# Feed-forward loop: gate and up groups alternate, both sums opened first, silu one unit later, one bank's scaling moved

## What is computed

```python
x = x + tanh(g_xattn) * xattn(layernorm(x), ctx, ctx, Wq, Wk, Wv, Wo, bo, g)
x = x + tanh(g_ffn) * ffn(layernorm(x), ...)
def ffn(x):                          # Wg, Wu: 512 x 1376, Wd: 1376 x 512, from 4-bit words
    gate, up = x2 @ Wg, x2 @ Wu      # w[k, n] = (q[k, n] - z[k // 128, n] - 1) * s[k // 128, n]
    return ((gate * sigmoid(gate) * up) @ Wd).astype(float16)
```

## Time and profile before

| | us |
|---|---|
| median of 3 runs (lowest, highest) | 684.23 (682.98, 684.38) |
| profiled execution, its own time | 683.05 |
| its span, first to last instruction | 681.3 |
| first gate job of unit 0, from the span's start | 410.24 |
| unit 2's first job | 421.84 |
| last gate or up job | 668.23 |

### The profile page before, as it was taken

The page is one execution under the profiler, slowest core; times in us unless marked ns, Lnnn a source line. Parts: engine busy times, 40 slices in busy tenths (PEclk is TensorE's granted clock), DMA queues, the critical chain, the costliest instruction groups (busy, mean ns, idle before and its releaser), DMA issues.

```text
span 681.3 us, 14346 instructions
## 1 busy us (share of the span) xinstructions
PE 662.0 (97%) x5097; PEld 341.9 (50%) x5097; DVE 586.5 (86%) x807; ACT 494.9 (73%) x872; POOL 257.9 (38%) x352
## 2 busy tenths in 40 slices
PE   7899999999999999999999998999999999999996
PEld 6454555455456455545645543444444444444443
DVE  7777898898889889889887948999979988998897
ACT  4886677678677667767866746877787877777774
POOL 6213323223232332322326364554434444444442
PEclk8999999999999999999999999999999999999999
DMA  4112330430332222032021000000000001000102
GB/s 116 37 51 55 99 82 22 102 96 8 97 95 51 53 81 79 7 84 79 10 79 22 7 8 1 1 1 0 1 32 31 1 0 46 18 0 17 43 4 62
DMA packets 30619, 28.58 MB, mean 42 GB/s; under 512 B 18623, under 2 KB 20810, under 8 KB 30578
## 3 DMA queue, kind: packets, MB, share of 16 engines
q1 hardware_dynamic: 28170, 27.37, 14.9%
q10 hardware_dynamic: 2408, 0.70, 0.4%
HBM read 22.06 MB, written 4.23 MB: 39 GB/s over the span
## 4 chain that ended last, share of the span: by engine, by line
PE 87%; ACT 5%; DVE 5%; issue 1%; POOL 1%; SPq 0%; DMA 0%; DVEq 0%; POOLq 0%
PE pair L1364 9%; PE small L1081 8%; PE small L1047 8%; PE pair L1153 8%; PE pair L1365 7%; PE pair L1033 6%; PE pair L1378 6%; PE pair L1387 6%; ACT eq L695 4%; PE small L1065 4%; PE small L1364 4%; PE small L1365 4%; PE pair L1178 3%; PE pair L1012 3%; PE small L1119 3%; PE pair L1163 2%
## 5 line engine op out<-in xcount | busy, mean ns | idle before, releaser
L1767 DVE SCALAR_TENSOR_TENSOR acc<-pair,scale_T,acc 128x512 f32<-128x512 f32 (+1 forms) x176 | 131.5, 748 | 17.6 <-ACT acc L830 5.0
L1378 PE MATMUL pair<-in_hi,d_int 128*128 128x512 f32 (+1 forms) x176 | 100.8, 575 | 0.6 <-ACT in_hi L845 0.5
L1387 PE MATMUL pair<-in_lo,d_int 128*128 128x512 f32 (+1 forms) x176 | 100.2, 573 | 0.0
L686 ACT ACTIVATE ek<-pair,kneg 128x512 f32<-128x512 f32 x128 | 86.5, 683 | 18.0 <-DVE kneg L1627 17.9
L594 POOL TENSOR_TENSOR inter<-act_gate,acc 128x512 f32<-128x512 f32 (+1 forms) x43 | 54.9, 1276 | 109.4 <-DVE acc L1767 104.0
L1364 PE MATMUL pair<-ek,w_gu 128*128 128x512 f16 (+1 forms) x235 | 91.3, 388 | 2.0 <-DVE acc L1767 1.3
L1365 PE MATMUL pair<-ekT,w_gu 128*128 128x512 f16 (+1 forms) x235 | 89.0, 379 | 0.0
L1632 DVE TENSOR_TENSOR eq<-eq,pair 128x1024 f32<-128x1024 f32 x64 | 77.8, 1216 | 11.1 <-PE pair L1138 10.8
L1622 DVE TENSOR_REDUCE qmax<-pair 128x16 f32<-128x1024 f32 x64 | 78.2, 1222 | 8.4 <-PE pair L1012 7.2
L856 ACT ACTIVATE pair<-pair,rescale 128x512 f32<-128x512 f32 x131 | 81.9, 661 | 0.8 <-PE pair L1387 0.8
L1627 DVE TENSOR_REDUCE kneg<-pair 128x2 f32<-128x1024 f32 x64 | 77.9, 1218 | 0.7 <-PE pair L1033 0.7
(11 more groups left out here) (198 smaller groups left out, 1346.2 us busy)
## 6 DMA issues: line engine op xcount, KB each, us to landing
xall<-in_x SPq DMA_DIRECT2D x16, 256.0 KB, 2.8
ctx_raw<-in_ctx SPq DMA_DIRECT2D x16, 256.0 KB, 3.0
out_x<-xall SPq DMA_DIRECT2D x16, 256.0 KB, 2.0
zero<-zeros_plus SPq DMA_DIRECT2D x8, 344.0 KB, 5.6
packed<-in_L_ffn_gate_qweight SPq DMA_DIRECT2D x4, 688.0 KB
packed<-in_L_ffn_up_qweight SPq DMA_DIRECT2D x4, 688.0 KB
packed<-in_L_ffn_down_qweight SPq DMA_DIRECT2D x10, 256.0 KB
zero<-zeros_plus SPq DMA_DIRECT2D x5, 256.0 KB, 4.6
```

What stands on the lines that cost most here:

```text
L686: act.activation(ek[:, b, t, :], k_pairs[t % 2][:, b, :], ACT.Exp, bias=kneg[:, b, t:t + 1], scale=-1.0, accum_out=ksum[:, k_slot(b, t):k_ ...
L1378: pe.matmul(z_bank[nt], d_int[0:w, it, nt * P:(nt + 1) * P], in_hi[0:w, n % 2, :], start=it == 0, stop=False, skip_group_check=True)
L1387: pe.matmul(z_bank[nt], d_int[0:w, it, nt * P:(nt + 1) * P], in_lo[0:w, n % 2, :], start=False, stop=True, skip_group_check=True).then_inc ...
L1767: dve.scalar_tensor_tensor(out=acc[0:w, n % 2, m, :], in0=gu_bank[(8 * n + job) % 3][0:w, :], scalar=scale_T[0:w, it, 4 * m + g:4 * m + g ...
```

## The change

On TensorE and VectorE the jobs alternate between gate and up (`g, m` instead of `m, g`), so that jobs 0 and 1 are the two that open a sum and jobs 2 to 7 are additions, each waiting for the addition two jobs before. ScalarE opens both sums first, then makes silu of the unit before (one unit later than it did), then bank 0, in_hi, banks 1 and 3. Bank 2 goes to VectorE in every unit. In the code that runs before the loop nothing changes; the semaphores' counts are adapted.

```diff
@@ -62,35 +62,14 @@
     return min(P, INTER - it * P)
 
 
-def vector_extra(n):
-
-    j, it = divmod(n, IT)
-    return j > 0 and 3 <= it < 3 + TPC
-
-
-def act_scales(n):
-
-    return BANKS if vector_extra(n + 3) else ACT_BANKS
-
-
-def act_scaled(n):
-
-    return sum(len(act_scales(m)) for m in range(n))
-
-
-def dve_scaled(n):
-
-    return NJ * n - act_scaled(n)
-
-
 def bank_products(n, nt):
 
     return NJ * n + (LAST_LOWS if n == UNITS - 1 else BANKS).index(nt) + 1
 
 
-def groups_done(n, job):
-
-    return 6 * n + job - (job > GH)
+def sums_done(n, job):
+
+    return 6 * n + job - 1
 
 
 def at_least(p, n):
@@ -307,13 +286,13 @@
 
             last = n - UNITS + 2
             if last >= 0 and nt in ((3, 2), (0, 2))[last]:
-                eng.wait_ge(z_dve, dve_scaled(UNITS - 2) + 2 * last + ((3, 2), (0, 2))[last].index(nt) + 1)
+                eng.wait_ge(z_dve, UNITS - 2 + 2 * last + ((3, 2), (0, 2))[last].index(nt) + 1)
             elif last >= 0:
-                eng.wait_ge(z_act, act_scaled(UNITS - 2) + 2 * last + ((0, 1), (3, 1))[last].index(nt) + 1)
-            elif nt in act_scales(n):
-                eng.wait_ge(z_act, act_scaled(n) + act_scales(n).index(nt) + 1)
+                eng.wait_ge(z_act, 3 * (UNITS - 2) + 2 * last + ((0, 1), (3, 1))[last].index(nt) + 1)
+            elif nt == 2:
+                eng.wait_ge(z_dve, n + 1)
             else:
-                eng.wait_ge(z_dve, dve_scaled(n) + 1)
+                eng.wait_ge(z_act, 3 * n + ACT_BANKS.index(nt) + 1)
 
         block = st.enter_context(nc.Block())
 
@@ -822,17 +801,17 @@
 
                 it = n % IT
                 w = width(it)
-                act.wait_ge(gu_mm, 8 * n + GH * m + 1)
+                act.wait_ge(gu_mm, 8 * n + m + 1)
                 if n >= 2 and m == 0:
                     act.wait_ge(gs_ready, n - 1)
                 elif n >= 2:
                     act.wait_ge(inter_ready, n - 1)
-                act.activation(acc[0:w, n % 2, m, :], gu_bank[(8 * n + GH * m) % 3][0:w, :], ACT.Copy,
+                act.activation(acc[0:w, n % 2, m, :], gu_bank[(8 * n + m) % 3][0:w, :], ACT.Copy,
                                scale=scale_T[0:w, it, 4 * m:4 * m + 1]).then_inc(s0_done, 1)
 
             def silu(n):
                 w = width(n % IT)
-                act.wait_ge(acc_done, 6 * n + 3)
+                act.wait_ge(acc_done, sums_done(n, 6))
                 if n:
                     act.wait_ge(inter_ready, n)
                 act.activation(act_gate[0:w, :], acc[0:w, n % 2, 0, :], ACT.Silu).then_inc(gs_ready, 1)
@@ -871,29 +850,30 @@
 
             for n in range(UNITS):
                 open_sum(n, 0)
+                open_sum(n, 1)
+                if n:
+                    silu(n - 1)
                 if late_input(n - 1):
                     transposed(late_input(n - 1))
-                if n:
-                    high_part(n - 1)
-                else:
+                if n == 0:
                     transposed(5)
                     transposed(6)
-                open_sum(n, 1)
+                    transposed(7)
+                if n == 1:
+                    step(PAIRS + 1, PAIRS // 2, 1, False, False, True, drain=True)
                 if n == 2:
                     act.wait_ge(ss_mm, PAIRS)
                     act.activation(ss_rows[:, :], small[1][:, 0:P], ACT.Copy).then_inc(ss_evac, 1)
                 bank_scaled(n - 2, 0)
-                silu(n)
-                if n == 0:
-                    transposed(7)
-                if n == 1:
-                    step(PAIRS + 1, PAIRS // 2, 1, False, False, True, drain=True)
+                if n:
+                    high_part(n - 1)
+                bank_scaled(n - 2, 1)
+                bank_scaled(n - 2, 3)
                 if n == 2:
                     act.activation(ident16[:, :], ident[:, :], ACT.Copy).then_inc(ident16_made, 1)
-                for nt in act_scales(n - 2)[1:]:
-                    bank_scaled(n - 2, nt)
                 if n in NORMALISED_IN:
                     ffn_normalised(NORMALISED_IN.index(n) + 2 * TPC)
+            silu(UNITS - 1)
             bank_scaled(UNITS - 2, 0)
             high_part(UNITS - 1)
             bank_scaled(UNITS - 2, 1)
@@ -1347,7 +1327,7 @@
             def gate_up(n, job):
 
                 j, it = divmod(n, IT)
-                w, (m, g) = width(it), divmod(job, GH)
+                w, (g, m) = width(it), divmod(job, 2)
                 if n == 0 and job == 0:
                     pe.wait_ge(w_int, PAIRS - 2)
                 if it == 0 and job == 0:
@@ -1355,10 +1335,10 @@
                 count = 8 * n + job
                 if count >= 3:
                     n_was, job_was = divmod(count - 3, 8)
-                    if job_was % GH == 0:
-                        pe.wait_ge(s0_done, 2 * n_was + job_was // GH + 1)
+                    if job_was < 2:
+                        pe.wait_ge(s0_done, 2 * n_was + job_was + 1)
                     else:
-                        pe.wait_ge(acc_done, groups_done(n_was, job_was))
+                        pe.wait_ge(acc_done, sums_done(n_was, job_was))
                 lhsT = w_gu[:, m, g, it * P:it * P + w]
                 rows = slice(j * CHUNK, (j + 1) * CHUNK)
                 pe.matmul(gu_bank[count % 3][0:w, :], lhsT, xT_hi[:, g, rows], start=True, stop=False)
@@ -1758,12 +1738,12 @@
 
             def add_group(n, job):
                 it = n % IT
-                w, (m, g) = width(it), divmod(job, GH)
+                w, (g, m) = width(it), divmod(job, 2)
                 dve.wait_ge(gu_mm, 8 * n + job + 1)
                 if g == 1:
                     dve.wait_ge(s0_done, 2 * n + m + 1)
                 else:
-                    dve.wait_ge(acc_done, groups_done(n, job) - 1)
+                    dve.wait_ge(acc_done, sums_done(n, job - 2))
                 dve.scalar_tensor_tensor(out=acc[0:w, n % 2, m, :], in0=gu_bank[(8 * n + job) % 3][0:w, :],
                                          scalar=scale_T[0:w, it, 4 * m + g:4 * m + g + 1], in1=acc[0:w, n % 2, m, :],
                                          op0=ALU.mult, op1=ALU.add).then_inc(acc_done, 1)
@@ -1839,10 +1819,9 @@
 
             for n in range(UNITS):
                 j, it = divmod(n, IT)
-                if 2 not in act_scales(n - 3):
-                    bank_scaled(n - 3, 2)
+                bank_scaled(n - 3, 2)
                 for job in range(8):
-                    if job % GH:
+                    if job >= 2:
                         add_group(n, job)
                     if n <= LATE_UNITS[-1] + 1:
                         rest_of_attention(n, job)
```

## The result

The changed kernel takes a median of 671.88 us (671.24 to 672.65, four runs) against 683.94 us for the kernel before on the same chip; the ratio is **0.9826** (95% interval 0.9809 to 0.9843), 12.1 us less. The prediction was 672.4 us. The changed kernel's profiled execution took 672.23 us, with a span of 670.2.

A forecast was written before the change was run, and what follows sets the result against it. VectorE's additions, waiting on its own last result, were taken to hold up TensorE. 12.7 - 1.9 = 10.8, plus 0.3 and 0.2, gives 11.3 us off: 671.75 from the profiled execution, 672.9 from the median, so 672.4; range 669.3 to 677.

The forecast's parts named there:

- The pool: Units 2 to 43: 246.4 us less 226.5 (jobs) and 7.2 (work between jobs) leaves TensorE held up 12.7 us.
- 1.9: Units 2 to 43: stalls expected to stay after the change, 1.9 us, bounds 0 and 6.
- The residual addition: VectorE, twelve units: a residual addition ahead delays the next addition, 0.09 us a unit, 1.1 us in all.
- The wait: VectorE additions to one sum: waiting for the one before costs 0.19 us, four times a unit; alternating makes it 0.
- Rival 1: VectorE: the 0.85 us spacing stays, the twelve units rise to 6.06 us, 1.3 to 7.9 us slower; 688 us, chance 0.06.
- VectorE's idle time: Sign in the feed-forward loop: VectorE's idle time goes up, most of it ahead of a unit's first addition; no size.
- The bank: Twelve units: the fourth bank's scaling adds 0.66 us each on VectorE, under TensorE's time; ScalarE's saving counted as nothing.
- ScalarE's order: ScalarE, each unit: both openings first and silu one unit later, counted at a cost of 0.
- The walk: Plain unit, ScalarE's start times: opening up 1.32 us, silu 1.91, bank 0 3.57, in_hi 4.15, bank 1 4.75.
- the two covers: ScalarE: 0.15 us between bank 3 and the next opening; a late opening reaches TensorE only after 0.6 us more.
- Rival 2: ScalarE becomes late, every unit pays 0.1 to 0.2 us and half the gain goes; 678 us, chance 0.14.
- The ends: Units 0 and 1: gain 0.3 us, bounds -0.3 and 1.5; end of the kernel: 0.2 us, bounds 0 and 0.35.

The follow-up runs named there:

- run 5: Changed kernel with output rows' transposes one job earlier and the residual addition ahead of the unit's first addition: 671.71 us, ratio 0.9816 to the kernel before.
- run 1: Changed kernel, but additions of jobs 4 to 7 wait for the addition right before instead of two before: 685.37 us, ratio 1.0014 to the kernel before.
- run 2: Kernel before, with only the fourth bank moved back to VectorE in the twelve units: 685.08 us, ratio 1.0005.
- run 4: Changed kernel, but the fourth bank stays on ScalarE in the twelve units: 672.22 us, ratio 0.9826 to the kernel before.
- run 6: Changed kernel, but silu at the end of its own unit, behind bank 3: 673.51 us, ratio 0.9839 to the kernel before.
- run 7: Changed kernel with one more unused copy on ScalarE behind bank 3 in units 3 to 43: 674.56 us, ratio 0.9853 to the kernel before.
- run 3: Gate and up alternate on TensorE and VectorE, but ScalarE keeps its old order: 731.11 us, ratio 1.0688 to the kernel before.

## Why the prediction was right

*The pool.* 12.7 us of hold-ups in units 2 to 43 by the earlier trace rows; 11.35 came back, so 235.04 - 226.5 - 7.2 = 1.3 us stay, where 1.9 was taken. The residual addition was to cost 0.09 a unit and costs 0.05 (run 5), 0.6 in all; another 0.13 stays at the end of units 10 and 21 each (last job 0.80 us), where the next chunk begins.

*The wait.* Shown by run 1: 0.19 us four times a unit, by the age of the value alone, since nothing else differs. Between additions it is 0.66 to 0.69 us where the value is old, 0.84 to 0.86 where it is the last instruction's. The Trainium skill, VectorE: DVE Perf Modes, section "The DRAIN you can't avoid", says of a chain of eight copies that "the semaphore costs nothing extra here"; as a rule on all waits, which the prediction weighed, that does not hold in run 1. The same section adds that "A next op that is not held starts earlier", which the prediction left out. Rival 1, the slower case, had its mechanism wrong. Run 1, which makes each wait a fresh one, shows its 6.06 us in nine of the twelve units, but in all only 1.0 us above the kernel before, just under its 1.3 to 7.9.

*VectorE's idle time.* The prediction called VectorE full before the change, and named a rise of its idle time as a sign. In units 2 to 43 that fell, from 27.4 us (246.39 less 218.95 busy) to 19.9 (235.04 less 215.17). Added up from the traces, 17.9 us of it before were gaps of about 0.10 us, nearly all ahead of additions that waited for the one right before; 0.8 us in such short gaps is left. The idle time ahead of a unit's first addition rose from 9.2 to 18.7 us, as forecast. So the sign holds for that part alone, and VectorE was not full before in the 21 units where it had those 9.2 us.

*The bank.* Counted at 0.66 us under cover on VectorE and at nothing on ScalarE. Runs 2 and 4: nearly nothing in the sum either way (0.4 and 0.25 us), but in the old order its place on ScalarE had cost as much as it saved on VectorE, which the prediction did not see: it put all of TensorE's hold-ups there down to VectorE.

*ScalarE's order.* The walk's times stand to 0.05 us in the trace, and the two covers (0.15 to the next opening, 0.6 by the banks' turn) are what runs 6 and 7 ran into. Run 3 shows that this part, counted at 0, is what makes the alternation possible. Rival 2 was nearer than its chance said in one respect: a single further half microsecond of ScalarE costs 1.7 us, two cost more than the change gained.

*The ends.* A gain of 0.35 us at the start where 0.3 was taken, and of 0.36 at the end where 0.2 was taken with a bound of 0.35: the last addition starts 0.64 us after its job (658.13 for 657.49), as in the walk.

*Against its own execution* the sum gave 671.75, and 672.23 came: 0.8 us more gain than summed in the feed-forward part, 0.96 lost to a later end of attention, the rest outside the span. That the forecast of 672.4 lies within 0.5 us of the median is closer than its terms were, and in part luck.

## What to carry to other kernels

Where one engine adds into the same tile again and again, read the start-to-start spacing of its instructions, not their durations: a chain on its own last result shows as a spacing longer than the instruction, and alternating two independent sums removes it without removing a wait. Before such a reordering, walk one unit of each engine in its queue's order: the neighbour whose results the new order wants earlier has to be reordered with it, or the loss is larger than the gain. Idle time of an engine that sits in a loop with another is not room for work; the length of the loop is what counts.

## What was not expected

The start of the feed-forward part moves from execution to execution, 410.24 to 413.08 us over these traces, though no run changed anything ahead of it; units 0 and 1 took 11.25 us in each of six kernels. By these six, a stage's window tells kernels apart to some 0.1 us where totals need 1 us and more; each kernel has one trace. What moves attention was not tried.

An engine's queue can turn a gain of 12 us into a loss of 47 with the same instructions (run 3), and a loss of 2.6 us on one engine can be hidden by the same loss on another (run 2).
